# A convolutional attention kernel: attention turned by transposing DMAs in place of TensorE transposes

## What is computed

```python
k = lax.conv_general_dilated(x, w1, padding=[(6, 6), (6, 6)], rhs_dilation=(2, 2), ...) + b1[None, :, None, None]
k = lax.conv_general_dilated(k, w2, ...) + b2[None, :, None, None]
attn = jax.nn.softmax(k, axis=1)
shifts = jnp.stack([xp[:, :, 2*u:2*u+64, 2*v:2*v+64] for u in range(7) for v in range(7)], axis=1)
x = jnp.einsum('bkchw,bkhw->bchw', shifts, attn)
...
y = jax.nn.gelu(yc.T[None, :, None, :] + x * D[None, :, None, None], approximate=False)
out = layernorm_over_channels(x + y) * ln_w + ln_b
```

## Time and profile before

| | before |
|---|---|
| median of 3 runs | 800.34 us (799.68 to 800.49) |
| the profiled execution's own time | 799.94 us |
| span of its instructions | 797.8 us |
| mean granted TensorE clock | 0.985 |
| TensorE busy | 744.9 us, 93% |
| VectorE busy | 673.8 us, 84% |
| ScalarE busy | 546.9 us, 69% |
| GpSimd busy | 193.8 us, 24% |
| DMA traffic | 58.60 MB, mean 73 GB/s |

### The profile page before, as it was taken

One profiled execution on the slowest core, in us unless ns is written; L12 is line 12 of the kernel. 1 busy time (PEld: TensorE's weight loads), 2 busy tenths in 40 slices (PEclk: granted clock), 3 DMA queues, 4 the chain that ended last, 5 costly groups with the idle time before them and its releaser, 6 DMA issues.

```text
span 797.8 us, 27596 instructions
## 1 busy us (share of the span) xinstructions
PE 744.9 (93%) x12338; PEld 446.7 (56%) x12338; DVE 673.8 (84%) x867; ACT 546.9 (69%) x903; POOL 193.8 (24%) x115
## 2 busy tenths in 40 slices
PE   4959989999999999999999999999999999999994
PEld 1525545675557545664567545664567545764681
DVE  0898997989889988989888988989888988686675
ACT  2874454757686786867686786687786677486566
POOL 5114113024311243024311341114301431013010
PEclk9969999999999999999999999999999999999998
DMA  9482223023714146224705255324704230414124
GB/s 298 134 140 34 42 54 56 2 42 55 150 27 94 28 86 116 55 43 79 145 6 95 40 105 83 72 35 86 133 3 94 45 78 3 92 28 71 28 55 106
DMA packets 266721, 58.60 MB, mean 73 GB/s; under 512 B 266265, under 2 KB 266346, under 8 KB 266346
## 3 DMA queue, kind: packets, MB, share of 16 engines
q1 hardware_dynamic: 138488, 40.79, 24.1%
q10 hardware_dynamic: 128114, 16.04, 13.0%
HBM read 40.04 MB, written 16.78 MB: 71 GB/s over the span
## 4 chain that ended last, share of the span: by engine, by line
PE 28%; DVE 21%; ACT 19%; issue 12%; ACTq 3%; POOL 3%; DVEq 0%; POOLq 0%
PE cv L526 15%; PE wk L575 7%; ACT V L913 5%; ACT chs L967 4%; DVE V L1435 3%; ACTq L957 3%; DVE o L1583 2%; POOL chs L417 2%; DVE tg L1577 2%; DVE Z L1476 2%; PE ms L606 2%; PE wk L596 2%; ACT tg L1002 2%; PE wk L634 1%; DVE Z L1485 1%
## 5 line engine op out<-in xcount | busy, mean ns | idle before, releaser
L526 PE MATMUL cv<-V,W 128*32 128x496 f16 (+6 forms) x7840 | 429.0, 374 | 6.3 <-issue 4.1
L526 PEld LDWEIGHTS cv<-V,W 128*32 128x32 f16 (+1 forms) x7840 | 198.3, 96 | 205.0 <-issue 18.2
L913 ACT ACTIVATE V<-R,sc 128x1024 f16<-128x1024 f32 (+1 forms) x88 | 109.9, 1277 | 61.6 <-DVE R L1361 50.3
L386 POOL TENSOR_TENSOR R<-raw 128x1152 f32<-128x1152 f32 x32 | 94.5, 2954 | 203.8 <-DVE V L1435 105.1
L1435 DVE SCALAR_TENSOR_TENSOR V<-R,sc,V 128x1024 f16<-128x1024 f32 (+1 forms) x88 | 115.1, 1327 | 3.0 <-ACT V L913 3.0
L596 PE MATMUL wk<-band,XT 128*128 128x209 f16 (+1 forms) x1080 | 87.7, 238 | 3.3 <-ACT o L989 3.0
L596 PEld LDWEIGHTS wk<-band,XT 128*128 128x128 f16 x1080 | 78.6, 97 | 15.0 <-ACT o L989 8.4
L575 PEld LDWEIGHTS wk<-AT,sel 128*128 128x128 f16 x2268 | 69.6, 100 | 15.0 <-issue 7.8
L411 POOL TENSOR_TENSOR chs<-o 128x1024 f32<-128x1024 f32 x14 | 45.2, 3226 | 130.0 <-DVE o L1583 121.0
L575 PE MATMUL wk<-AT,sel 128*128 128x16 f16 (+1 forms) x2268 | 73.9, 190 | 0.1
L1361 DVE SCALAR_TENSOR_TENSOR R<-R 128x1024 f32<-128x1024 f32 (+1 forms) x56 | 68.6, 1257 | 0.0
(11 more groups left out here) (194 smaller groups left out, 909.8 us busy)
## 6 DMA issues: line engine op xcount, KB each, us to landing
raw<-in_x_dram SPq DMA_DIRECT2D x16, 1024.0 KB, 11.5
out_dram<-o SPq DMA_DIRECT2D x28, 512.0 KB, 4.6
AT<-in_x_dram ACTq DMA_DIRECT2D x82, 128.0 KB, 3.0
w1raw<-in_L_conv_w_dram SPq DMA_DIRECT2D x2, 3136.0 KB, 16.7
xs<-in_x_dram ACTq DMA_DIRECT2D x40, 128.0 KB, 3.0
out_dram<-o SPq DMA_DIRECT2D x8, 256.0 KB, 3.9
AT<-in_x_dram SPq DMA_DIRECT2D x4, 128.0 KB, 3.0
xs<-in_x_dram SPq DMA_DIRECT2D x2, 128.0 KB, 3.6
```

Source lines behind the costliest of these rows:

```text
L386: nc.gpsimd.tensor_tensor(R[buffer][:, :, :, :], rows_of(par, j + 2), rows_of(par, j), ALU.subtract).then_inc(pool_rows, 1)
L526: ins = pe.matmul(to.rearrange("p (w t c) -> p w t c", w=2, c=COLS)[:, :, :, c0:c1], W[:, ws, h * K7 + v, k0:k1], slot(n, a)[:, low, :, t0 ...
L913: nc.scalar.activation(v_array(n, a, 0), array(a), ACT.Identity, scale=sc[:, par, 3:4]).then_inc(vhi, 1)
```

## The change

In units 1 to 7 (for m = 0 to 6) the 16 transposes on TensorE and the two copies on ScalarE are gone. SyncE's queue issues two transposing DMAs per unit in their place, one for each column parity `w`: each reads 128 partitions x 1024 fp16 values of `HL` (256 KB) and writes the eight turned 128x128 blocks to `AT`. They count up a new semaphore, `att_in`.

- SyncE waits for the whole of `HL` (`soft`), for the turned x tiles of the unit before (`xt_done`), and for the spreads that read the last contents of `AT` (`sel_done`).
- TensorE waits before the first spread for both DMAs, by `att_in`, where it waited for ScalarE's copies.
- ScalarE waits before the next write of `HL` for the DMAs that read it.
- `mean(m, 0)` takes over the wait for `normed` that stood in `turn_attention`.
- In SyncE's list the stores of a unit's second half move behind the next unit's transposing DMAs.
- The last unit keeps its transposes on TensorE and its copies.

```diff
--- before.py
+++ after.py
@@ -218,7 +218,6 @@
         ms = ctx.enter_context(nc.psum_tensor("ms", [P, 2, BANK], F32))
         cv = ctx.enter_context(nc.psum_tensor("cv", [P, 4, BANK], F32))
         wk = ctx.enter_context(nc.psum_tensor("wk", [P, 2, BANK], F32))
-        ms16 = ms[:].bitcast(F16)
         cv16 = cv[:].bitcast(F16)
 
         last_banks = [wk[:, 0, :], wk[:, 1, :]] + [cv[:, i, :] for i in range(4)]
@@ -263,6 +262,7 @@
         amax_part, amax_all, scale_steps = sem("amax_part"), sem("amax_all"), sem("scale_steps")
         row_made, pool_rows, vhi, vlo = sem("rows_made"), sem("pool_rows"), sem("v_high"), sem("v_low")
         conv_done, z_evac, z_step = sem("block_convolved"), sem("sums_copied"), sem("logit_steps")
+        at_in = sem("att_in")
         lt_ready, soft, exp_done = sem("logits_turned"), sem("softmax_steps"), sem("exp_done")
         hl_hi, ht_ready, at_copy = sem("att_high"), sem("att_turned"), sem("att_copied")
         sel_done, bhi, blo = sem("band_spread"), sem("band_high"), sem("band_low")
@@ -350,6 +350,15 @@
                 sp.wait_ge(pool_rows, POOL_ROWS * n)
                 sp.wait_ge(xt_done, 8 * n)
                 load(n + 1, 1 - par, b)
+
+            def turn_attention(m):
+                sp.wait_ge(soft, SOFT * m + SOFT)
+                sp.wait_ge(xt_done, STAGES * (m + 1))
+                if m:
+                    sp.wait_ge(sel_done, STEPS * m)
+                for w in range(2):
+                    sp.dma_start_transpose(AT[:, w, PAD:PAD + ROWS, :].rearrange("p (t r) c -> p t (r c)", r=4),
+                                           HL[:, w * WIN:(w + 1) * WIN].rearrange("p i k -> p (i k)")).then_inc(at_in, 16)
 
             sp.dma_start(w2raw[:, :], w2.rearrange("k m a b -> k (m a b)")).then_inc(s_w2, 16)
             for h in range(HALVES):
@@ -364,10 +373,13 @@
             load(1, 1, 0)
             next_load(1, 1, 1)
             for n in range(1, UNITS):
+                turn_attention(n - 1)
+                if n > 1:
+                    store(n - 1, (n - 1) % 2, (n - 2) // 2, 1)
                 store(n, n % 2, (n - 1) // 2, 0)
                 if n < UNITS - 2:
                     next_load(n + 1, (n + 1) % 2, (n + 2) // 2)
-                store(n, n % 2, (n - 1) // 2, 1)
+            store(UNITS - 1, (UNITS - 1) % 2, (UNITS - 2) // 2, 1)
             for i in range(QUARTERS):
                 for h in range(HALVES):
                     sp.wait_ge(q_done[h], i + 1)
@@ -546,18 +558,12 @@
                                        Z[:, w, t].rearrange("p k c -> p (k c)"), id32[:, :])
                 ins.then_inc(lt_ready, 1)
 
-            def turn_attention(m, g):
-                pe.wait_ge(soft, SOFT * m + SOFT)
-                pe.wait_ge(normed, 4 * m + 4)
-                for t in range(4):
-                    for w in range(2):
-                        c = w * 4 * P + t * P
-                        ins = pe.transpose(ms16[:, g, c:c + P], HL[:, w * WIN + 4 * g + t, :], id16[:, :])
-                ins.then_inc(ht_ready, 1)
-
             def spread(m, r):
                 if r == 0:
-                    pe.wait_ge(at_copy, 2 * m + 2)
+                    if m == LAST:
+                        pe.wait_ge(at_copy, 2)
+                    else:
+                        pe.wait_ge(at_in, 32 * m + 32)
                 banks = 6 if m == LAST else 2
                 if r >= banks:
                     pe.wait_ge(blo, 10 * m + r - banks + 1)
@@ -609,8 +615,8 @@
 
             def mean(m, q):
                 pe.wait_ge(os_made, 2 * m + q + 1)
-                if q:
-                    pe.wait_ge(normed, 4 * m + 6)
+                if q or m:
+                    pe.wait_ge(normed, 4 * m + (6 if q else 4))
                 sums_of_columns().then_inc(mean_done, 1)
 
             def variance(m, q):
@@ -643,8 +649,6 @@
                 conv(n, 3, 5)
                 turn_logits(m, 1)
                 conv(n, 5, 19)
-                turn_attention(m, 0)
-                turn_attention(m, 1)
                 conv(n, 19, 21)
                 spread(m, 0)
                 spread(m, 1)
@@ -969,12 +973,9 @@
 
             def attention_high(m):
                 act.wait_ge(soft, SOFT * m + 10)
+                if m:
+                    act.wait_ge(at_in, 32 * m)
                 nc.scalar.copy(HL[:, :, 0:TAPS], E[:, :, :]).then_inc(hl_hi, 1)
-
-            def turned_attention(m, g):
-                act.wait_ge(ht_ready, 2 * m + g + 1)
-                nc.scalar.copy(AT[:, :, PAD + 16 * g:PAD + 16 * g + 16, :].rearrange("p w r c -> p w (r c)"),
-                               ms16[:, g, :].rearrange("p (w f) -> p w f", w=2)).then_inc(at_copy, 1)
 
             def band_high(m, r):
                 act.wait_ge(sel_done, 10 * m + r + 1)
@@ -1046,8 +1047,6 @@
                 exponentials(m, 8, 16)
                 v_high(n, par, 6)
                 attention_high(m)
-                turned_attention(m, 0)
-                turned_attention(m, 1)
                 v_high(n, par, 7)
                 v_high(n, par, 8)
                 band_high(m, 0)
@@ -1277,10 +1276,11 @@
 
             def last_high(w):
                 act.wait_ge(l_soft, (14, 19)[w])
+                act.wait_ge(at_in, 32 * m)
                 nc.scalar.copy(HL[:, w * WIN:(w + 1) * WIN, 0:TAPS], E[:, w * WIN:(w + 1) * WIN, :]).then_inc(l_hi, 1)
 
             def last_turned(w):
-                act.wait_ge(ht_ready, 2 * m + w + 1)
+                act.wait_ge(ht_ready, w + 1)
                 nc.scalar.copy(AT[:, w, PAD:PAD + ROWS, :].rearrange("p r c -> p (r c)"), cv16[:, 2 + w, :]).then_inc(
                     at_copy, 1)
 
```

## The result

The changed kernel takes **816.22 us** (median of 4 runs, 815.25 to 816.88), against 800.41 for the kernel before: slower by a ratio of 1.0197, 95% interval 1.018 to 1.0215. The forecast was 825, with a range of 804 to 855. The profiled execution took 815.97 us with a span of 814.2, 16.4 us longer than before.

The account below looks back on a forecast made before the run. TensorE, busy 93% of the span, was taken as the bound, with 3.20 us from `HL` to first spread to beat. 799.94 + 19.6 (late spreads) - 2.8 (ScalarE credit) + 8.5 (clock) = 825.2, said as 825 us, range 804 to 855.

Parts of the forecast that it names:

- The point of no loss: From `HL` ready to TensorE's first spread: the old path takes 3.20 us, which the DMAs have to beat.
- The landing, 6.0 us: After `HL` is ready, the DMA pair was to land in 6.0 us; as plain copies 5.0, at best 4.2.
- The term of 19.6 us: First spread 2.8 us late in each of 7 units, from a landing at 6.0 against 3.20: +19.6 us.
- The credit of 0.4 us per unit: ScalarE's copies gone, its first band copy no longer keeps VectorE waiting: 7 x 0.4, or -2.8 us.
- The clock, five falls of 1.7 us: TensorE's clock halves for some 3.4 us after the standstill, 1.7 us lost in 5 of 7 units: +8.5 us.
- Edits at no price: SyncE's stores moved behind the transposing DMAs, and the added or moved waits, were to hold nothing up: no cost.
- Signs: In the changed profile: TensorE wait about 4 us, seven clock dips, band copy right behind the spread, units near 91.5 us.
- slow turning: Rival: DMAs turn in 32-byte pieces, landing takes some 16 us; +99 us, 899 us in all; chance 0.09.
- block by block: Rival: the DMAs turn the 16 blocks one after another, 48 us; +323 us, 1123 us in all; chance 0.03.
- value by value: Rival: no crossbar transfer, 262144 pieces take 213 us per unit; some 2270 us in all; chance 0.02.
- Faster: Rival: the landing beats TensorE's old path, below 3.6 us after `HL`; 795 or 790.5 us; chance 0.05.
- Absorption: Rival: TensorE, late at the spread, makes it up from at most 2.7 us idle per unit; 800 us; chance 0.06.

Follow-up runs that it names:

- mixed kernels: Kernel before with `HL` in halves, first half by one transposing DMA, second by 8 TensorE transposes: 799.89 us; with 120 one-column matmuls at the start 797.87 us.
- split kernel: Changed kernel with `HL` written in two halves and each transposing DMA issued when its half is ready: 809.18 us, ratio 1.0101.
- shifted kernel: 48 one-column matmuls added at the start of the kernel turning one parity by DMA, the other on TensorE (808.76 us): 801.69 us, ratio 1.0016.

## Why the prediction was right, and where its sizes were off

- **The point of no loss, 3.20 us after `HL`, and that the DMAs miss it**: right, in all seven units.
- **The landing, 6.0 us**: 4.5 to 5.0 measured. The term of 19.6 us was mis-sized; it measured 10.0. The store's 4.6 us with an issue of 0.37 was taken for the pair, and 1 us was added for slower turning. In fact turning runs at full rate, the first issue takes 1.3 us, the two transfers 2.8 and the rest 0.5. That 4.5 lies between the prediction's 4.2 and 5.0 for plain copies is in part luck, since its parts are other ones. The page of the kernel before had a nearer row than the 512 KB store, one of the size of each DMA, which with 0.37 us gives 4.3:

```profile
out_dram<-o SPq DMA_DIRECT2D x8, 256.0 KB, 3.9
```

  The upper end of the range, 9.5 us, stands in the prediction without a working; the latest spread of the changed kernel came at 4.98.
- **The credit of 0.4 us per unit**: too high by the traces. From the first pair of spreads to the fifth the kernel before takes 14.2 to 14.3 us, and the changed one without a fall of the clock 14.1, so 0.1 to 0.2 us per unit, 1 us in all. The run times can't tell it: the run with idle matmuls has spreads 10.6 us later in all and lost 8.0 to 9.4 us, with an interval of some 3 us. ScalarE's freed 1.9 us were of little use, since it then waited 2.24 us for VectorE.
- **The clock, five falls of 1.7 us**: six falls of 0.9 by the traces, 1.1 by the medians. That it falls was right, the price per fall was too high, because the spreads do not slow down at half clock. Together 5.6 to 6.4 us against 8.5. The mean clock of 0.969 met the foretold 0.97 in part by luck: seven falls in the units were foretold and six came, and the trace has one more than before at the start (26.9 us) and one more in the tail (777.8).
- **Edits at no price**: right. The order of SyncE's list and the traffic cost nothing measurable.
- **Signs**: the standstill is 2.6 to 3.1 us, not 4, and a unit 90.2 us, not 91.5. The first band copy does follow its spread at once, as foretold: it starts 1.06 us after the spread does, where it was 1.79.
- **Rivals**: slow turning, block by block and value by value are refuted by 204 to 223 GB/s. Faster would have needed a landing under 3.6 us, and two issues and one transfer alone take longer (1.3 + 1.3 + 1.4 us). Absorption was a small part, as above. The 1309 ns for a 128x128 block that the prediction takes from the Trainium skill (VectorE: DVE Perf Modes, § The three transpose paths) is no price per block here: 8 blocks land 3.2 us after the issue, 1.4 of it the transfer. A single block was not run.

The sum by terms read from the traces is 10.0 - 1.0 + 5.6 = 14.6 us, against a measured 15.8. The rest of 1.2 us was not placed. The two profiled spans differ by 0.8 us before the first `HL` already, where the kernels do the same.

## What to carry to other kernels

Before a step goes from a busy engine to a DMA, compare latencies at the step's consumer, not the work saved: the 1.0 us of TensorE and 1.9 us of ScalarE per unit were cheaper than a DMA path of 4.5 to 5.0 us with 1.9 us of cover. A stall costs more than its length if the clock falls behind it, and a few idle matmuls inside the wait took that part away here. Where a transposing DMA must be on such a path, do not cut it into so many that their issues take longer than their transfers, and start it from the first part of the data that is ready. One DMA for all 16 blocks was not run; if its issue took 1.3 us too, the first spread would start 1.3 + 2.8 + 0.5 = 4.6 us after `HL` by the parts above, an estimate, no sooner than with the two.

## What was not expected of the hardware

- A transposing DMA holds the issuing queue 1.25 to 1.3 us whether it has 4 or 8 blocks, and its data start 1.2 to 1.3 us after the issue begins; a plain store's issue took 0.37 us. Every issue of 1.5 to 2.4 us in these traces had an instruction fetch beside it.
- A 16 KB fetch of instructions that starts 1.1 to 2.8 us after the issue delays 8 blocks' landing from 3.1 to as much as 4.9 us: the whole transposing transfer stands still beside it in the trace shown, where a plain load went on. In the mixed kernels fetches at 2.46, 2.87 and 2.90 us did no harm, so the end of the harmful stretch is not sharp. An unrelated change in the number of TensorE's instructions moves these collisions, and was worth 7 us in one kernel.
- The spreads, 56 matmuls of 16 columns with a weight load each, took 1.9 us at 2.4 GHz and at 1.2 GHz, while 20 convolution matmuls went from 1.26 to 2.1 and 2.3 us.
- The clock fell at standstills of 2.6 to 3.1 us in six cases of seven, and behind waits of 1.9 us in four of the five units of the split kernel that had them; in the shifted kernel a wait of 2.03 us in unit 4 brought no fall. Why some were spared was not tested.
